# A mixture-of-experts stage cut into two parts: 41 expert blocks of the first six groups are started among the last group's steps

## The reference, cut to what matters

```
logits = flat @ gate_W + gate_b                 # 8 experts
top_v, top_i = top_k(logits, 2); w = softmax(top_v)
for e in range(8):
    mid = gelu(flat @ exp_W1[e] + exp_b1[e])    # 128 -> 512, exact gelu
    y_e = mid @ exp_W2[e] + exp_b2[e]           # 512 -> 128
    out = out + w_full[:, e:e+1] * y_e
```

## Time and profile before

| | |
|---|---|
| median of three runs | 587.75 us |
| the profiled execution | 587.89 us |
| its span, first to last instruction | 586.1 us |
| TensorE busy | 482.7 us (82%) |
| VectorE busy | 400.0 us (68%) |
| ScalarE busy | 283.8 us (48%) |
| GpSimd busy | 325.9 us (56%) |
| mean granted TensorE clock | 0.899 |
| moved by DMA | 47.70 MB |

### The profile page before, as it was taken

The page is one execution under the profiler, slowest core; times in us unless marked ns, Lnnn a source line. Parts: engine busy times, 40 slices in busy tenths (PEclk is TensorE's granted clock), DMA queues, the critical chain, the costliest instruction groups (busy, mean ns, idle before and its releaser), DMA issues.

```text
span 586.1 us, 13689 instructions
## 1 busy us (share of the span) xinstructions
PE 482.7 (82%) x4384; PEld 404.4 (69%) x4384; DVE 400.0 (68%) x1239; ACT 283.8 (48%) x686; POOL 325.9 (56%) x349
## 2 busy tenths in 40 slices
PE   3365799999999999999999999862099999999920
PEld 2253577777777777777777777742099999999920
DVE  5765867989799899799799796434245555555526
ACT  3213536556456457357466375412065665565510
POOL 4614626636856877777776758525335555545520
PEclk9766899899899999899999999665599999999975
DMA  4920100100100200200000000000376767777639
GB/s 95 214 74 0 36 3 1 37 2 1 51 15 11 56 10 12 56 11 10 20 20 1 21 19 19 20 19 28 110 217 187 220 197 202 216 210 210 190 109 323
DMA packets 57851, 47.70 MB, mean 81 GB/s; under 512 B 15407, under 2 KB 44466, under 8 KB 57781
## 3 DMA queue, kind: packets, MB, share of 16 engines
q1 hardware_dynamic: 53460, 38.35, 24.4%
q0 software_dynamic: 4320, 8.47, 4.2%
HBM read 35.18 MB, written 12.08 MB: 81 GB/s over the span
## 4 chain that ended last, share of the span: by engine, by line
PE 47%; DVE 25%; issue 9%; POOL 8%; DVEq 4%; DMA 3%; SPq 2%; ACT 2%; POOLq 0%
PE bank L705 11%; PE bank L715 11%; PE bank L446 4%; POOL sorted_rows L1109 3%; PE bank L520 2%; DVE mx L1399 2%; PE bank L525 2%; PE bank L373 2%; DVE places L1367 2%; PE bank L547 2%; PE bank L439 2%; DVE places L1276 2%; DVE vbd L1388 2%; PE bank L430 2%; POOL rs L973 2%
## 5 line engine op out<-in xcount | busy, mean ns | idle before, releaser
L1168 POOL DMA_INDIRECT result_rows<-back,rows x71 | 69.4, 978 | 76.9 <-DVE back L1625 74.8
L948 ACT ACTIVATE mid<-bank,b 128x128 f32<-128x128 f32 x284 | 81.0, 369 | 52.3 <-PE bank L705 52.3
L1109 POOL DMA_INDIRECT sorted_rows<-send,slot_u x64 | 64.0, 1000 | 29.2 <-issue 14.4
L1091 POOL TENSOR_TENSOR km<-kb,head 128x512 f32<-128x512 f32 x56 | 58.1, 1041 | 38.4 <-ACT kb L818 24.1
L705 PE MATMUL bank<-hT,w 128*128 128x128 f32 x568 | 76.6, 279 | 0.2 <-DVE hT L1615 0.2
L547 PEld LDWEIGHTS bank<-vbd,pT 128*128 128x128 f32 x512 | 65.4, 197 | 14.0 <-issue 6.4
L715 PE MATMUL bank<-w,mid 128*128 x568 | 74.9, 275 | 0.0
L547 PE MATMUL bank<-vbd,pT 128*128 128x36 f32 x512 | 66.6, 277 | 5.3 <-DVE places L1411 2.4
L705 PEld LDWEIGHTS bank<-hT,w 128*128 128x128 f32 x568 | 70.4, 195 | 0.4 <-DVE hT L1615 0.4
L715 PEld LDWEIGHTS bank<-w,mid 128*128 128x128 f32 x568 | 68.9, 192 | 0.0
L520 PE MATMUL bank<-km,qbd 128*128 128x512 f32 x128 | 68.0, 614 | 0.0
(11 more groups left out here) (202 smaller groups left out, 972.0 us busy)
## 6 DMA issues: line engine op xcount, KB each, us to landing
w<-in_L_ffn_exp_W_dram SPq DMA_DIRECT2D x79, 256.0 KB, 3.5
rows<-sorted_rows SPq DMA_DIRECT2D x71, 65.0 KB
places<-result_rows SPq DMA_DIRECT2D x16, 256.0 KB
places<-in_x_dram SPq DMA_DIRECT2D x8, 256.0 KB, 2.9
places<-in_ctx_dram SPq DMA_DIRECT2D x8, 256.0 KB, 3.3
out_dram<-acc SPq DMA_DIRECT2D x8, 256.0 KB, 5.7
result_rows<-back,rows POOLq DMA_INDIRECT x71, 3.2
sorted_rows<-send,slot_u POOLq DMA_INDIRECT x64, 2.4
```

The source lines that it names most:

```text
L948: A(mid[s][:, c, :], hidden[2 * s + c // 2][:, c % 2 * P:c % 2 * P + P], ACT.Gelu, bias=b1[:, bass.ds(expert, 1), c]).then_inc(mid_ok, 1)
L1091: G.tensor_tensor(km[n % 2][:, :, :], kb[u][:, n % 2, t * S:t * S + S].unsqueeze(1).broadcast_to([P, HG, S]), head8[:, :].unsqueeze(2).bro ...
L1109: G.indirect_dma_start(out=sorted_dram, out_offset=bass.IndirectOffsetOnAxis(ap=slot_u[u][:, j // 2, t:t + 1], axis=0), in_=send[u][:, t, ...
L1168: G.indirect_dma_start(out=result_dram, out_offset=bass.IndirectOffsetOnAxis(ap=rows[s][:, D:D + 1].bitcast(U32), axis=0), in_=back[s % 4] ...
```

## The change

The stage of expert blocks is cut in two parts, and everything around it is moved to fit.

1. **Two parts of the table.** After six groups (`FIRST = 6`) the rows are counted once more: `count_rows(0)` on TensorE in beat 10, and behind `attended(6, 2)` on VectorE the new functions `count_blocks(0)`, `whole_blocks`, `first_table` and `segments`. Of the full blocks that six groups are sure to give, whatever the routing (`SURE` = 41), the first table is made. The second table (30 blocks) is made after block 9 (`count_blocks(1)`), block 11 (`second_lengths`) and block 14 (`second_table`). `y_T(6)` on TensorE now waits until the count of beat 10 has been read out of `end_bank`.
2. **Blocks 0 to 7 among the last group's steps.** TensorE runs block 0 ahead of `y_T(7)`, block 1 ahead of `project_out(7)`, blocks 2 to 4 ahead of `a_T(7)`, block 5 ahead of `gate_logits(7)`, blocks 6 and 7 ahead of `ranks(7)`. The other engines have them at the corresponding places. GpSimd's eight transfers of `scatter(7)` now stand in pairs between the result transfers of blocks 7 to 11.
3. **PSUM.** The turned rows have one bank instead of two (`turned = bank[0]`), the results banks 1 and 3.
4. **Zeros behind the regions.** They are written ahead of the loads of block 33, with the eight places read by one group of register loads.
5. **Results of six groups under the blocks.** When block i's loads (62 to 67) are issued, the two result loads of group i-62 follow on SyncE's queue. Groups 0 to 3 are added behind blocks 65, 67, 69 and 70 on VectorE and stored; groups 4 to 7 are added at the end, and only the results of groups 6 and 7 are loaded there.
6. **Start.** The load of group 1's inputs stands behind two of the eighteen small weight loads instead of behind all. Some semaphores between two VectorE instructions became `drain`.

The diff, cut to its core:

```diff
+    FIRST = 6
     BLOCKS = (2 * TOKENS + E * (P - 1)) // P
+    SURE = -((E * (P - 1) - 2 * FIRST * N) // P)
+    WHOLE = (2 * FIRST * N + E * (P - 1)) // P
+    PART_BLOCKS = (SURE, BLOCKS - SURE)
...
@@ SyncE
-                for dst, src in other_weights:
+                for dst, src in other_weights[0:2]:
                     sp.dma_start(dst, src).then_inc(w_loaded, 16)
                 load(1, 1)
+                for dst, src in other_weights[2:]:
+                    sp.dma_start(dst, src).then_inc(w_loaded, 16)
...
+                for i in range(BLOCKS):
+                    if i == 0:
+                        wait_part(0)
+                        sp.wait_ge(moe_loaded, (2 * E + 2) * 16)
+                    if i == PART_BLOCKS[0] - RING:
+                        blank_tails()
+                    if i == PART_BLOCKS[0]:
+                        wait_part(1)
...
+                    load_block(i, experts[i - at], places_of[i - at])
+                    if WHOLE + RING - 1 <= i < WHOLE + RING - 1 + FIRST:
+                        load_results(i - WHOLE - RING + 1)
+
+                for g in range(FIRST - 2):
+                    store(g)
                 for s in range(RING):
                     sp.wait_ge(returned[s], ((BLOCKS - 1 - s) // RING + 1) * 16)
...
+                for g in range(FIRST, GROUPS):
+                    load_results(g)
+                for g in range(FIRST - 2, GROUPS):
+                    store(g)
@@ TensorE
                     if k >= 1:
                         pe.wait_ge(rank_ok, k)
+                    if k == FIRST:
+                        pe.wait_ge(table, 2)
                     transposes(end_bank, y[k % 2]).then_inc(yT_ps, 1)
...
-                turned, hidden, result = bank[0:2], (bank[2], bank[4], bank[5], bank[6]), (bank[3], bank[7])
+                turned, hidden, result = bank[0], (bank[2], bank[4], bank[5], bank[6]), (bank[1], bank[3])
...
+                        if b - 5 == GROUPS - 1:
+                            blocks(2, 5)
                         a_T(b - 5)
...
+                        if b - 5 == FIRST - 1:
+                            count_rows(0)
                         scores(b - 3, 0)
...
+                blocks(8, 8 + 2)
+                count_rows(1)
+                blocks(8 + 2, BLOCKS)
@@ ScalarE
+                        if b - 4 == GROUPS - 1:
+                            blocks(1, 3)
                         a_normal(b - 4)
...
+                        if b - 4 == GROUPS - 1:
+                            blocks(3, 5)
                         copy_h2T(b - 4)
...
                         second_copy(b - 4)
+                        if b - 4 == GROUPS - 1:
+                            blocks(5, 7)
                         exp_gap(b - 4)
@@ GpSimd
+                        if b - 4 == GROUPS - 1:
+                            blocks(2, 8)
                         scatter(b - 4, 0)
...
+                        if b - 3 == GROUPS - 1:
+                            blocks(0, 2)
                         a_scale(b - 3)
@@ VectorE
+                late = (BLOCKS - 6, BLOCKS - 4, BLOCKS - 2, BLOCKS - 1)
+
+                def add_results(g):
+                    dve.wait_ge(y_loaded[g // 3], 32 * len([h for h in ALL if h // 3 == g // 3]))
+                    dve.wait_ge(res_ok, g + 1)
+                    V.tensor_tensor(acc[:, g, :, :], acc[:, g, :, :], first[2 * g], ALU.add)
+                    dve.drain()
+                    V.tensor_tensor(acc[:, g, :, :], acc[:, g, :, :], first[2 * g + 1], ALU.add).then_inc(out_ok, 1)
...
                         attended(b - 4, 2)
+                        if b - 5 == FIRST - 1:
+                            count_blocks(0)
+                            whole_blocks()
+                            first_table()
+                            segments()
...
+                blocks(8, 8 + 2)
+                count_blocks(1)
+                blocks(8 + 2, 8 + 4)
+                second_lengths()
+                blocks(8 + 4, 8 + 7)
+                second_table()
+                blocks(8 + 7, BLOCKS)
+                for g in range(FIRST - 2, GROUPS):
+                    add_results(g)
```

More of the change, by code:

```diff
@@ new lines, in output @@
+                def output(i, expert):
+                    s = i % RING
+                    if i >= 2:
+                        pe.wait_ge(y2_ok, i - 1)
+                    for c in range(CH):
+                        pe.wait_ge(mid_ok, CH * i + c + 1)
+                        last = pe.matmul(result[s % 2][:, 0:D], mid[s % 2][:, c, :],
+                                         w2[:, bass.ds(expert, 1), c, :].rearrange("p o d -> p (o d)"),
+                                         start=c == 0, stop=c == CH - 1)
+                    last.then_inc(y2_ps, 1)
@@ L710, in output @@
-                def output(i, s, expert):
-                    if i >= 2:
-                        pe.wait_ge(y2_ok, i - 1)
-                    for c in range(CH):
-                        pe.wait_ge(mid_ok, CH * i + c + 1)
-                        last = pe.matmul(result[s % 2][:, 0:D], mid[s % 2][:, c, :],
-                                         w2[:, bass.ds(expert, 1), c, :].rearrange("p o d -> p (o d)"),
-                                         start=c == 0, stop=c == CH - 1)
-                    last.then_inc(y2_ps, 1)
@@ L1164, in _ @@
                     beat(b)
[L1166 to L1173 removed]
+                blocks(11, BLOCKS)
             @block.vector
```

406 lines of the change are left out of this document (252 added, 154 removed).

## The result

The changed kernel took 591.22 us (median of 20 runs, 584.44 to 595.89) where the kernel before took 587.12 (20 runs, 581.13 to 593.52): ratio 1.0079, interval 1.0046 to 1.0112. The ratio leaves out the executions of both kernels that were slow as a whole, so it is not the quotient of the two medians (1.0070). The changed kernel is 0.8% slower, which by the prediction's bound of 1% is no change; the forecast was 577, the range 568 to 587. The profiled execution took 591.45 us with a span of 589.6, against 587.89 and 586.1.

What follows compares the result with a forecast made beforehand. Bounds: TensorE fully used in expert blocks, a latency chain ending the beats, a tail of memory traffic and additions. -2 + 8 - 9.6 - 7.5 = -11.1 gives 576.8 profiled, 577 as median; range 568 to 587.

Steps and rivals of the forecast that it cites:

- Start, -2: Early beats: group 1's inputs issued behind two weights let GpSimd start earlier, -2 us, bounds 0 and -4.
- Beat 10, +8: First table's 21 VectorE instructions stop TensorE for 6.0 us, and half clock loses 2; bounds 4 and 11.
- 4 us of half clock, which lose 2: Beat 10: TensorE's clock at 0.50 for 4 us behind the first table's stop, costing 2 us.
- Rival 3: Three stalls (beat 10, `output(3)`, second table) each cost 5.5 us in half clock: 585, range 582 to 593.6; chance 0.20.
- From 388.1 to the last product, 163.3: Last attention product's end to last block's product: 172.9 us before, 163.3 after, or -9.6.
- The five steps, the waits among them and their share of the half clock: After 388.1: last group's steps 3.7 us at full clock, waits among them 9.9; the stage's half clock 12 us, losing 6.
- VectorE in blocks 9 to 17, 5: Second table's pieces on VectorE cost 4.1 us, GpSimd's transfers 1 more: 5, bounds 2 and 8.
- GpSimd backlog, 1 more: Blocks 7 to 10: 12 transfers and the scatter on GpSimd exhaust the `back` buffers about block 13, 1 us more.
- Zeros, 1.5: Ahead of block 33: eight writes at about half of 8.43 us on SyncE, 2.5 covered: 1.5, bounds 0 and 6.
- Results and additions, 3: Result loads under blocks 62 to 67 and four additions cost TensorE 3 us, bounds 1 and 7.
- Tail, -7.5: After the last product: four result loads instead of sixteen, 25.1 us before, 17.6 after; bounds -6.5 and -9.
- The rule of the Trainium skill: ScalarE's two added table switches: with drains they would cost 2.8 us more than the 1.3 taken, about 579.5.

Runs made afterwards that it cites:

- the first lot: Lot on a 588.2 us chip; its run meant here: changed kernel with the first table in six pieces behind group 7's maxima, ratio 0.9880 to the kernel before.
- that of the fourth: Lot on a 589.0 us chip; its run meant here: the same kernel with the first table in six pieces once more, ratio 0.9939 to the kernel before.
- the five edits: Changed kernel, first part ending at block 40, zeros and both tables spread, scatters one in three blocks: 0.9729 on a 589.0 us chip, 1.0047 at 601.5.
- two, three and four edits: Changed kernel with cut at 40 and first table spread: 1.0028; zeros spread too: 1.0021; second table spread too: 0.9884; ratios to the kernel before.

## Why the prediction was wrong

**Start, -2:** right as far as can be told (2.1 by one pair of traces; 0.4% by itself on the kernel before).

**Beat 10, +8: measured 12.5; the stop right, the clock wrong.** The stop was forecast at 6.0 and is 5.77, with the instructions as counted. The term that failed is "4 us of half clock, which lose 2". From 350 to 388 the kernel before has clock 1.00 and then 0.70 over 20 us, a loss of 6.0 us at full clock. The changed kernel loses 0.24 of 12 us and 0.50 of 20 us behind the stop, 12.9: 7 more, not 2. The clock fell twice. Directly behind the stop it cost 2.9 us, about as forecast. The miss is the second fall, from about 377 on, behind the short wait of the earlier trace rows that the kernel before has too: this time it stayed down to the end of the beats, and the prediction has no term for that.

That the stop made this second fall longer is not shown. It stays down to the end of the beats in all five traces that have the stop, on chips of 587 to 589 us. But the kernel with the first table spread, which has no long stop, shows both lengths in its two traces. First the one of the first lot, then that of the fourth:

```profile
370.00:380.00 10.00, 10.00 (x41) 8.28 (x40) 4.76 (x29) 3.47 (x7) 4.29 (x4) 0.51 0.28 78
380.00:388.00 8.00, 6.59 (x46) 5.29 (x45) 3.07 (x19) 2.84 (x5) 3.75 (x4) 0.91 0.41 127
```

```profile
370.00:380.00 10.00, 10.00 (x38) 8.11 (x39) 4.00 (x19) 3.66 (x7) 4.73 (x5) 0.50 0.24 66
380.00:394.00 14.00, 12.65 (x54) 10.12 (x52) 4.37 (x29) 2.95 (x5) 3.86 (x4) 0.50 0.28 86
```

So spreading the table gave 10.6 us back in one trace and 6.1 in the other, and the difference is this fall. Rival 3, the clock eats the gain, had the right place, and what the clock took here beyond the sum was 5 us of the rival's 8.5. That the measured 591.2 lies within that rival's 582 to 593.6 is luck in part, since the register loads below brought as much.

**From 388.1 to the last product, 163.3: wrong by 11.1.** Term by term:
- The five steps, the waits among them and their share of the half clock were 3.7, 9.9 and part of the 6: measured 15.6. Right. The wait at `output(3)` was put at 4.6 and is 2.9.
- VectorE in blocks 9 to 17, 5: measured 6.8 with its half clock. Right in size; the "GpSimd backlog, 1 more" was mis-sized, since it alone holds blocks 18 to 22 by 4.5 us once the table is gone (second table spread).
- Zeros, 1.5: measured 4.8. The eight writes took 5.44 us, where about 4 were expected. The step that failed is "a weight load is issued 6 us ahead, so 2.5 are covered": SyncE loads rows behind the zeros too, and TensorE waited 2.83 us for rows, and then ran at half clock.
- Results and additions, 3: measured 3.6, and 2.9 as the difference of two kernels. Right.
- **No term at all: the register loads, 6.3.** The second part's first block is 41, and the prediction took its loads to cost nothing, as in the kernel before. The table moved by one element shows the cost by itself, 15 us for eight boundaries; cut at 40 it is gone.

The rest of the sum is not confirmed by this. Cut at 40, the stretch takes 168.9 us (400.71 to 569.57), still 5.6 above the forecast. The kernel with the five edits needs 162.1 us from its first `rows_T` to the last product, close to 163.3, but by luck: its edits also take away most of the 5 us for VectorE that the sum contains (6.8 became 1.4 between blocks 10 and 20), and other terms are larger than forecast.

**Tail, -7.5:** -8.4 in the changed kernel, 7.1 as the difference of two kernels. Right.

**The rule of the Trainium skill,** "ScalarE: Activation LUTs", section What ACT_TABLE_LOAD costs, with a drain of about 1380 ns in each switch, was not the cause. The trace of the changed kernel has no room for one at the two added loads:

```profile
426.35 1.28 ACT L937 ACT_TABLE_LOAD   x1
428.16 0.20 ACT L937 ACTIVATE dlt<-dlt 128x4 f32<-128x4 f32 x1 [0.53 <-DVE dlt L1542]
428.38 1.28 ACT L948 ACT_TABLE_LOAD   x1
429.68 2.17 ACT L948 ACTIVATE mid<-bank,b 128x128 f32<-128x128 f32 x8
```

The second load starts 0.02 us behind the exponential, and the Gelu 0.02 us behind the load. Behind the first, the exponential waits 0.53 us for VectorE.

**What stays open.** The five edits' ratio is 3.2% higher on one of the chips of 600 us than on one of 589, and the kernels with two, three and four edits stand on such chips 2 to 3% above the sums that were expected of them. The traces tie the stops to runs of indirect transfers, whose end VectorE follows by 0.88 to 0.97 us in six cases and by 0.65 to 1.36 in others, and the same run does no harm on the chip of the result. Why chips differ in this is open. No kernel was run there with GpSimd's transfers kept apart, so this is read, not shown. Open is also how long TensorE's clock stays at 0.50 in beat 10: two traces of one kernel differ by more than 10 us in it.

## What to carry to other kernels

A part of a table that is loaded into registers in groups should begin at a multiple of the group, also when the amount of work says one element more. (Only starts one element behind such a multiple were measured.) Work that is put in front of a busy engine's only supplier costs its own length and some half clock behind it, so it belongs in pieces behind the supplier's own steps; and a wait that is taken away must be followed to the next cause of the same wait, as with the second table and the scatters. A plan that fills the idle engine of one chip should be tried on a second chip before its gain is believed.

## What was not expected of the hardware

- A load of eight 32-bit numbers from one partition into an engine's registers takes 0.52 to 0.93 us if it begins at element 0, 8, 16 or so on, and 1.66 to 2.33 us if it begins at 1, 9, 17 and so on, 41, 49 or 57, on TensorE, VectorE, ScalarE and SyncE alike. The last seven, begun at 64, took 0.96 to 1.13 us in the kernel before.
- After a wait of 1.7 us (2.5 with the first table spread) TensorE's granted clock went to 0.50 and stayed there through nearly full work (10.00 of 10 us busy), for about 10 us in some executions and to the end of the beats, 20 us and more, in others. Two traces of one kernel show one length each.
- On three of five chips TensorE's ends reached VectorE and ScalarE 1 to 2 us late and more while GpSimd issued indirect transfers with 0.3 us between them. With 0.9 us between them no such delay is seen on one of these chips (95.00 of 95 us busy), and on the chips of 587 and 589 us VectorE started 0.14 and 0.15 us behind the product in the midst of such a run.
